# Attention kernel: both halves of each head's share are added by VectorE, and ScalarE copies five of eight turned tiles instead of four

## What is computed

```python
scores = jnp.einsum('bhqd,bhkd->bhqk', q, k) * SCALE
p = jnp.maximum(bias_p, 0.01)
a = jnp.maximum(bias_a, 0.01)
dist = jnp.abs(pos[None, :] - pos[:, None])
kb = -p * jnp.log1p(a * dist)
attn = jax.nn.softmax(scores + kb[None], axis=-1)
out = jnp.einsum('bhqk,bhkd->bhqd', attn, v)
out = out.transpose(0, 2, 1, 3).reshape(Bb, Ss, H * D)
return out @ out_w.T
...
x = x + s * g
```

## Time and profile before

| | us |
|---|---|
| median of 3 executions | 1762.97 |
| lowest and highest of them | 1758.57, 1763.05 |
| the profiled execution | 1762.45 |
| its span | 1760.7 |
| attention of layer 0 with all stages running, within the span | about 440 to 1500 |

### The profile page before, as it was taken

One profiled execution on the slowest core, in us unless ns is written; L12 is line 12 of the kernel. 1 busy time (PEld: TensorE's weight loads), 2 busy tenths in 40 slices (PEclk: granted clock), 3 DMA queues, 4 the chain that ended last, 5 costly groups with the idle time before them and its releaser, 6 DMA issues. The chain is left out here.

```text
span 1760.7 us, 39221 instructions
## 1 busy us (share of the span) xinstructions
PE 1627.8 (92%) x12064; PEld 893.6 (51%) x12064; DVE 1491.2 (85%) x3046; ACT 1179.4 (67%) x1807; POOL 1414.3 (80%) x820
## 2 busy tenths in 40 slices
PE   5879989857999999999999999999999999689998
PEld 3435654423555555555555555555555555345666
DVE  8779978996988989898898989898898989578666
ACT  6536434536878778777877878787877877644341
POOL 6667846857999999999999999999999999553445
PEclk9899999988999999999999999999999999899999
DMA  5467856768989989889889889989989988500110
GB/s 167 148 181 193 228 149 168 196 199 192 178 190 220 189 176 232 181 185 229 181 189 219 189 177 221 193 184 211 197 189 199 211 176 172 123 18 1 31 31 25
DMA packets 735171, 296.46 MB, mean 168 GB/s; under 512 B 630192, under 2 KB 697778, under 8 KB 735104
## 3 DMA queue, kind: packets, MB, share of 16 engines
q1 hardware_dynamic: 732304, 292.17, 73.7%
q0 software_dynamic: 2048, 3.15, 1.0%
q10 hardware_dynamic: 768, 0.53, 0.1%
HBM read 101.34 MB, written 58.85 MB: 91 GB/s over the span
## 5 line engine op out<-in xcount | busy, mean ns | idle before, releaser
L1271 POOL TENSOR_TENSOR probs_lo<-probs 128x1024 bf16<-128x1024 f32 x512 | 954.0, 1898 | 80.2 <-ACT probs L1235 79.7
L1235 ACT ACTIVATE probs<-scores,neg_max 128x1024 f32<-128x1024 f32 x512 | 588.3, 1149 | 219.9 <-DVE neg_max L1153 211.2
L1153 DVE CUSTOM_DVE_ANT_0 scores<-score_ps,bias_tab 128x1024 f32<-128x1024 f32 x512 | 620.5, 1220 | 76.8 <-issue 69.7
L1067 PE MATMUL score_ps<-x 128*128 128x512 bf16 x1024 | 308.5, 383 | 31.3 <-PEq L294 17.8
L1083 PEld LDWEIGHTS turn_ps<-ident_bf,probs 128*128 128x128 bf16 x4096 | 261.3, 98 | 146.0 <-issue 55.9
L1083 PE MATMUL turn_ps<-ident_bf,probs 128*128 128x128 bf16 x4096 | 314.0, 220 | 0.2
L1102 PE MATMUL pv_ps<-probs_t_hi,v_hi_lo 128*128 128x512 bf16 x1024 | 263.6, 380 | 0.3 <-DVE share L1185 0.3
L1242 ACT COPY probs_t_hi<-turn_ps 128x1024 bf16<-128x1024 bf16 x256 | 254.1, 993 | 0.0
L439 POOL TENSOR_TENSOR qk_parts<-rotated,qk_parts 128x1024 bf16<-128x1024 f32 x64 | 137.6, 2154 | 87.5 <-ACT qk_parts L872 86.7
L1168 DVE COPY probs_t_hi<-turn_ps 128x1024 bf16<-128x1024 bf16 x256 | 172.7, 675 | 0.8 <-PE turn_ps L1083 0.8
L1588 POOL TENSOR_TENSOR q_state<-state,q_t 128x1024 f32<-128x1024 f32 x32 | 75.7, 2367 | 108.5 <-PE s_ps L1766 68.4
(11 more groups left out here) (236 smaller groups left out, 2316.2 us busy)
## 6 DMA issues: line engine op xcount, KB each, us to landing
x<-qk_parts SPq DMA_DIRECT2D x192, 256.0 KB, 3.3
qk_parts<-qk_parts SPq DMA_DIRECT2D x252, 128.0 KB
v_hi_lo<-v_parts SPq DMA_DIRECT2D x64, 256.0 KB, 3.1
bias_tab<-bias_by_distance SPq DMA_DIRECT2D x64, 240.0 KB, 3.7
v_parts<-bias_tab SPq DMA_DIRECT2D x52, 256.0 KB
probs_t_lo<-probs_lo SPq DMA_TRANSPOSE x512, 3.2
v_stacked<-v_three SPq DMA_DIRECT2D x72, 32.0 KB, 2.0
g<-in_x SPq DMA_DIRECT2D x4, 512.0 KB, 6.1
```

Source lines behind the costliest of these rows:

```text
L1067: pe.matmul(sp_[n % 2][:, cs], QB[s][:, q], KK[s][:, cs], start=True, stop=False)
L1153: v.tensor_tensor_reduce(SB[n % 2][:], sp_[n % 2][:], TB[s][:, j:j + S], -SCALE, 3.0e38, ALU.add, ALU.min, neg_max[:, n % 16:n % 16 + 1]). ...
L1235: act.activation(PR[n % NP][:], SB[n % 2][:], ACT.Exp, bias=neg_max[:, m:m + 1], scale=-1.0, accum_out=row_sum[:, m:m + 1]).then_inc(exped, 1)
L1271: g.tensor_tensor(LQ[n % NL][:], PR[n % NP][:], PRB[n % NP], ALU.subtract).then_inc(low_made, 1)
```

## The change

VectorE no longer makes the tile `share`. It scales and adds each half with four `scalar_tensor_tensor`: the first half at `j = 7`, where `scale_share` was, the second half at `j = 0` (one step earlier than before, where it was `j = 1`). GpSimd adds nothing and only makes low halves. The semaphore `added` and the tile `share` go. Tile 1 of each head's turned tiles is copied by ScalarE in place of VectorE, in the step `j = 0`.

```diff
-    DVE_TILES, ACT_TILES = (1, 3, 5, 6), (0, 2, 4, 7)
+    DVE_TILES, ACT_TILES = (3, 5, 6), (0, 1, 2, 4, 7)
...
-            def scale_share(it, hh):
+            def add_share(it, hh, c):

                 h = hh % 2
-                v.wait_ge(recip, at(it, 2, hh + 1))
-                v.wait_ge(op_ready, at(it, 4, 2 * hh + 1))
-                v.wait_ge(added, at(it, 2, hh + 1))
-                v.tensor_tensor(SH[:], ov[0][:], last_axis(inv[:, BT * h:BT * h + 4], D), ALU.mult).then_inc(scaled, 1)
...
-                    ins = v.scalar_tensor_tensor(out=acc, in0=ov[1][:, k, :], scalar=inv[:, BT * h + 4 + k:BT * h + 5 + k],
+                    ins = v.scalar_tensor_tensor(out=acc, in0=ov[c][:, k % 4, :], scalar=inv[:, BT * h + k:BT * h + k + 1],
                                                  in1=acc, op0=ALU.mult, op1=ALU.add)
...
-                if there(n - BT) and j == 1:
-                    add_share(it, hh - 1)
+                if there(n - BT) and j == 0:
+                    add_share(it, hh - 1, 1)
...
                 if there(n) and j == PROJ_STEP:
-                    scale_share(it, hh)
+                    add_share(it, hh, 0)
...
-                g.tensor_tensor(acc, acc, SH[:], ALU.add).then_inc(added, 1)
...
-                if there(u) and u % BT == BT - 1:
-                    add_share(it, u // BT)
```

More of the change, by code:

```diff
@@ L936, in attend @@
     pv_ready, ot_ready, op_ready = sem("pv_ready"), [sem(f"ot_ready{c}") for c in range(2)], sem("op_ready")
-    scaled, added, add_begun = sem("scaled"), sem("added"), sem("add_begun")
+    scaled, add_begun = sem("scaled"), sem("add_begun")
     recip = sem("recip")
@@ L950, in attend @@
     OL = [sb(f"out_t_lo{i}", [P, CH], BF16) for i in range(2)]
-    SH = sb("share", [P, 4, D])
     ot_hi = [sem(f"ot_hi{c}") for c in range(2)]
@@ L969, in copied @@
         done, tiles = (hi_dve, DVE_TILES) if by_dve(n) else (hi_act, ACT_TILES)
-        eng.wait_ge(done, at(it, BT, n // BT * (BT // 2) + tiles.index(n % BT) + 1))
+        eng.wait_ge(done, at(it, 2 * len(tiles), n // BT * len(tiles) + tiles.index(n % BT) + 1))
     NI = B * G
@@ L1163, in untile @@
             def untile(it, n):
-                if n % BT == 1 and not (isinstance(it, int) and it == 0 and n < U):
+                if n % BT == DVE_TILES[0] and not (isinstance(it, int) and it == 0 and n < U):
                     v.wait_ge(pv_ready, at(it, 2, n // BT - 1))
@@ L1177, in take_out @@
                                     ALU.subtract).then_inc(ot_ready[c], 1)
-            def scale_share(it, hh):
+            def add_share(it, hh, c):
                 h = hh % 2
-                v.wait_ge(recip, at(it, 2, hh + 1))
-                v.wait_ge(op_ready, at(it, 4, 2 * hh + 1))
-                v.wait_ge(added, at(it, 2, hh + 1))
-                v.tensor_tensor(SH[:], ov[0][:], last_axis(inv[:, BT * h:BT * h + 4], D), ALU.mult).then_inc(scaled, 1)
[L1187 to L1193, removed]
+                v.wait_ge(op_ready, at(it, 4, 2 * hh + c + 1))
+                if c == 0:
+                    v.wait_ge(recip, at(it, 2, hh + 1))
+                v.wait_ge(scaled, at(it, 4, 2 * hh + c + 1))
+                for k in range(4 * c, 4 * c + 4):
+                    row = (it % B) * BT + k
                     acc = K.SACC[:, row, :] if isinstance(row, int) else K.SACC[:, bass.ds(row, 1), :].rearrange("p o d -> p (o d)")
-                    ins = v.scalar_tensor_tensor(out=acc, in0=ov[1][:, k, :], scalar=inv[:, BT * h + 4 + k:BT * h + 5 + k],
+                    ins = v.scalar_tensor_tensor(out=acc, in0=ov[c][:, k % 4, :], scalar=inv[:, BT * h + k:BT * h + k + 1],
                                                  in1=acc, op0=ALU.mult, op1=ALU.add)
@@ L1283, in step @@
                     low(it, u + LT)
-                if there(u) and u % BT == BT - 1:
-                    add_share(it, u // BT)
-            g.nop().then_inc(added, 1)
             run(g, step)
```

## The result

| | before | after |
|---|---|---|
| median of 3 executions, us | 1762.97 | 1782.25 |
| lowest and highest | 1758.57, 1763.05 | 1781.18, 1785.92 |
| the profiled execution | 1762.45 | 1785.92 |
| its span | 1760.7 | 1784.2 |

The ratio is 1.0122, 95% interval 1.0103 to 1.0142. The kernel became 19.3 us slower, where 19.6 were forecast.

The account below looks back on a forecast made before the run. A loop between VectorE and TensorE was taken to bound the kernel. 62 heads at 0.31 us (19.2) plus 0.43 at the attention's end gave 19.6 on 1762.97, so 1782.6 us, range 1768 to 1804.

Parts of the forecast that it names:

- The loop between VectorE and TensorE sets the head: Attention: `scores` needs `biased` of two tiles before, `bias_max` needs finished scores; this sets the head's 17.19 us.
- GpSimd's relief is worth nothing: Attention: GpSimd loses 1279 ns a head, but waits for ScalarE and nobody waits for it, so no gain.
- One sign: Trace after the change: GpSimd should show no addition and wait for ScalarE at nearly every tile.
- ScalarE's fifth copy is covered: Step `j = 0`: ScalarE gains a 0.992 us copy a head, within 3.3 idle; no transpose waits, cost nothing.
- The first half's additions fit into an idle of 0.43 with 0.07 to spare: At `j = 7`: four additions worth 1.04 us replace the scaling, done before `bias_max` of tile 4; cost nothing.
- The second half costs 0.31 a head: At `j = 0`: additions replacing a copy delay `bias_max` of tile 5 by 0.43; 62 heads pay 19.2 us.
- the slack: Before the scores of tile 7: TensorE could have started them 0.12 us earlier, so that much delay is free.
- The end of the attention pays 0.43 more: Last head: nothing overlaps there, so additions in place of a copy cost 1.04 - 0.61 = 0.43 us more.
- the upper price of the additions: Rival, 19%: both groups of four additions cost 1.23 us, so 0.62 a head, 39 in all, 1802.
- the absorbed delay: Rival, 11%: VectorE's idle of 1.07 before the next head is free time and swallows the 0.31; 1763.
- GpSimd as the bound: Rival, 9%: GpSimd sets the head, so its relief saves 0.48 us a head, 30 us in all; 1733.
- the engines lock each other out: Rival, 3%: one group of VectorE additions a head waits out a GpSimd low half, 118 us more; 1881.

Follow-up runs that it names:

- tile 1 alone: Kernel before, with tile 1 copied by ScalarE in place of VectorE, nothing else changed: 1762.34 us, ratio 0.9996.
- the pure move: Kernel before, with its four second-half additions moved from `j = 1` to `j = 0`, VectorE keeping the copy of tile 1: 1820.65 us, ratio 1.0329.
- the doses: Four kernels with two, three, four additions, or four and the copy, between `bias_max` of tiles 4 and 5: 0, 0.069, 0.326, 0.926 us a head more.
- tile 5 alone: Kernel before, with tile 5 copied by ScalarE in place of VectorE: 1725.32 us, ratio 0.9791.
- tiles 5 and 6: Kernel before, with tiles 5 and 6 both copied by ScalarE, VectorE keeping 1 and 3: 1757.57 us, ratio 0.9982.

## Why the prediction was right

The time was 1782.25 and the forecast 1782.6. Point by point:

- *The loop between VectorE and TensorE sets the head.* Shown by both signs: four additions put in behind `bias_max` of tile 4, which start that of tile 5 1.02 later, cost 0.93 a head, 0.61 taken out between tiles 0 and 1 brings 0.56. The same 0.61 taken out between tiles 4 and 5 brings nothing.
- *GpSimd's relief is worth nothing.* Shown by itself at 93% busy, and together with VectorE's additions at 96%. One sign was forecast wrongly: GpSimd waits for ScalarE at three tiles of eight and not at nearly every one.
- *ScalarE's fifth copy is covered.* Shown by the run with tile 1 alone.
- *The first half's additions fit into an idle of 0.43 with 0.07 to spare.* The stage with them at `j = 7` is 1094.5 against 1094.4. Their price of 1.04 was the right end of its bounds; the pure move showed it without a wait in the way.
- *The second half costs 0.31 a head.* Measured 0.326 over the stage. In the head shown the stall is 0.31 as forecast; the doses put the slack at 0.10 and not 0.12. Over 62 heads the 0.016 make 1.0 us. The remark beside this term, that VectorE's work in a head stays the same, doesn't follow from its numbers (2.26 against 2.08, 0.18 less); nothing in the sum rests on it.
- *The end of the attention pays 0.43 more.* It pays 0.40: from the last `bias_max` to the start of the instruction behind the multiplication it is 1514.57 - 1496.74 = 17.83 before and 1535.08 - 1516.85 = 18.23 after. But the term was right by luck, since two effects that it doesn't hold nearly cancel. First, `by_v` of the last head waits until the first half of the share before has been read, and here nothing hides that. Before, then after:

```profile
1503.51 3.61 PE L1102 MATMUL pv_ps<-probs_t_hi,v_hi_lo 128*128 128x512 bf16 x16 [0.26 <-DVE share L1185]
...
1524.00 3.61 PE L1101 MATMUL pv_ps<-probs_t_hi,v_hi_lo 128*128 128x512 bf16 x16 [0.64 <-DVE s L1188]
```

It starts 6.77 after the last `bias_max` before and 7.15 after: 0.38 later. Second, the view of VectorE after, at the end:

```profile
1531.75 2.16 DVE L1188 SCALAR_TENSOR_TENSOR s<-pv_ps,inv_sum,s 128x128 f32<-128x128 f32 x8 [0.34 <-PE pv_ps L1120]
1533.83 1.22 DVE L1214 TENSOR_TENSOR scores<-s,g 128x1024 f32<-128x1024 f32 x1
```

The additions do take eight instructions where a scaling and four stood, 2.08 us to the next start in place of 1.66. But the multiplication behind them takes 1.22, where it took 1.56 in the earlier trace rows, a gain of 0.34. With 0.06 that the eight start sooner after `by_v`, this is 0.38 + 0.42 - 0.34 - 0.06 = 0.40.

Of the rivals, the upper price of the additions, the absorbed delay and GpSimd as the bound are each answered by a run. That the engines lock each other out is answered by the view of the additions' line above: 512 of them between 340 and 351 ns, beside a GpSimd at work most of the time.

The hit within 0.4 us of the median is partly luck. The traces give 20.2 in the stage and 0.4 at the end, 20.6 together, where 19.6 were forecast; the medians of three executions each differ by 19.3, and the lowest and highest of the kernel before lie 4.5 us apart. The stage is the better test, with 20.2 measured and 19.2 forecast.

## What to carry to other kernels

When two engines hand tiles to each other in a loop, an instruction's price depends on which hand-over it stands in front of: the same copy, taken off the same engine, was worth 0 us between one pair of tiles and 35 between another. Before moving work, find for each place how long after an instruction's result its consumer starts in the trace, and take off what the hand-over takes where the consumer had been waiting (here 0.06 us from the end of VectorE's read to the matmul). What is left, here 0.10 to 0.12 us, may be put there free, and everything above it is paid once per round. And look at the engine which receives the work in the same way: with tile 5's copy on it ScalarE still stood idle 12% of the time, about 2 us a head, yet one more copy in front of the wrong cast cost 0.46.

## What was not expected of the hardware

The multiplication at the end of the attention, which reads two 128x1024 tiles in SBUF, took 1554 to 1557 ns in the five profiled kernels where GpSimd's last addition ran beside it (the one before, the pure move, tile 1 alone, tile 5 alone, tiles 5 and 6), and 1215 or 1216 in the other eight, where it did not. Two of them, before and with GpSimd's addition left out, in the groups by line, and GpSimd's last addition before, in the timeline:

```profile
L1221 DVE TENSOR_TENSOR scores<-s,g 128x1024 f32<-128x1024 f32 x1 | 1.6, 1556 | 0.0
...
L1220 DVE TENSOR_TENSOR scores<-s,g 128x1024 f32<-128x1024 f32 x1 | 1.2, 1215 | 0.0
...
1512.19 1.26 POOL L1279 TENSOR_TENSOR s<-s,share 128x512 f32<-128x512 f32 x1 [7.37 <-DVE share L1185]
```

The two touch different rows of the accumulator, the first batch's and the last's, so it isn't a wait for data. GpSimd's addition ends at 1513.45, 0.47 us after the multiplication's start at 1512.98, and the multiplication takes 0.34 longer.

The four-instruction additions, which read one tile in PSUM and one in SBUF and a scalar for each partition, showed no such stretch. The Trainium skill's page "SBUF — State Buffer", section "SBUF: two separate sides", names the pairing, a VectorE instruction with two SBUF inputs against a GpSimd one that reads SBUF, as a case in which one of them is blocked. The rows agree on which instruction is touched and which is not. Whether it was blocked whole for the rest of GpSimd's addition, as the page says, these times can't tell: the stretch of 0.34 is most of the 0.47 beside it, not all.
